# A graph layer on one core: banks of their own for spread scores and turned probabilities, sums one step later, expansion three steps ahead

## What is computed

```python
h = relu(layernorm(x))                     # 6250 nodes, 256 features
q, k, v = h @ wq + bq, h @ wk + bk, h @ wv + bv
scores = sum(q[dst] * k[src], -1) / 16 + (edge_weight * we + be)   # 200000 edges, sorted by dst
attn = softmax of scores over the edges of one dst
out = segment_sum(v[src] * attn, dst)
y = layernorm(h + out + h @ ws + bs)       # with g1, b1
return x + layernorm(y + ffn(y))           # with g2, b2
```

## Time and profile before

| | us |
|---|---|
| median of 3 runs | 2336.25 (2335.91 to 2336.41) |
| span of the profiled execution | 3211.3 |

### The profile page before, as it was taken

One profiled execution on the slowest core, in us unless ns is written; L12 is line 12 of the kernel. 1 busy time (PEld: TensorE's weight loads), 2 busy tenths in 40 slices (PEclk: granted clock), 3 DMA queues, 4 the chain that ended last, 5 costly groups with the idle time before them and its releaser, 6 DMA issues. The chain is left out here.

```text
span 3211.3 us, 68474 instructions
## 1 busy us (share of the span) xinstructions
PE 2427.3 (76%) x14747; PEld 1996.1 (62%) x14748; DVE 1767.6 (55%) x7372; ACT 1193.2 (37%) x2930; POOL 1635.5 (51%) x1828
## 2 busy tenths in 40 slices
PE   7577677777777777777777777777777777778998
PEld 5455556556555556565656566665666666657897
DVE  7454455555555545554555555555555555556787
ACT  6333333333333333333333333333333333334666
POOL 5355565555555545555554555555555445441154
PEclk8898899899899989998998999899988899999999
DMA  7233333333233323333233333332333233222222
GB/s 231 76 103 103 99 105 101 103 98 107 90 100 100 96 86 101 97 98 96 90 102 92 96 90 96 96 98 87 96 96 100 87 92 95 83 93 71 82 74 68
DMA packets 148148, 311.29 MB, mean 97 GB/s; under 512 B 33566, under 2 KB 84625, under 8 KB 148104
## 3 DMA queue, kind: packets, MB, share of 16 engines
q0 software_dynamic: 75264, 205.62, 21.5%
q1 hardware_dynamic: 54718, 90.19, 8.6%
q10 hardware_dynamic: 18122, 14.96, 1.5%
HBM read 290.21 MB, written 20.43 MB: 97 GB/s over the span
## 5 line engine op out<-in xcount | busy, mean ns | idle before, releaser
L488 POOL DMA_INDIRECT work<-h_rows,idx x1536 | 1457.3, 949 | 1339.9 <-SPq L372 956.2
L1079 PE MATMUL bank<-work 128*128 x3520 | 939.0, 412 | 24.5 <-issue 17.7
L1011 PE MATMUL bank<-q,onehot 128*128 x5304 | 804.6, 291 | 1.2 <-DVE work L832 0.7
L1079 PEld LDWEIGHTS bank<-work 128*128 128x128 f32 x3520 | 700.1, 211 | 146.8 <-issue 45.2
L886 DVE CUSTOM_DVE_ANT_0 work<-bank,work 128x512 f32<-128x512 f32 x440 | 330.5, 751 | 778.7 <-remote 476.4
L622 ACT COPY work<-bank 128x256 f32<-128x256 f32 x880 | 295.0, 376 | 1182.6 <-remote 812.8
L832 DVE SCALAR_TENSOR_TENSOR work<-bank,work 128x257 bf16<-128x257 f32 x1764 | 651.6, 425 | 143.5 <-PE bank L1011 44.2
L1017 PE MATMUL bank<-ident,work 128*128 128x128 f32 x1764 | 307.4, 302 | 500.5 <-ACT work L622 313.3
L1011 PEld LDWEIGHTS bank<-q,onehot 128*128 128x128 bf16 x5304 | 549.5, 104 | 85.4 <-issue 1.7
L1017 PEld LDWEIGHTS bank<-ident,work 128*128 128x128 f32 x1764 | 212.8, 148 | 578.0 <-ACT work L622 442.4
L1066 PE MATMUL bank<-ident,work 128*128 128x128 f32 x1760 | 283.6, 285 | 191.8 <-ACT work L619 182.8
(11 more groups left out here) (195 smaller groups left out, 1519.5 us busy)
## 6 DMA issues: line engine op xcount, KB each, us to landing
dst_words<-dst_short SPq DMA_DIRECT2D x99, 512.0 KB
work<-h_rows,idx POOLq DMA_INDIRECT x1568
bias<-h_rows ACTq DMA_DIRECT2D x56, 128.0 KB
r_rows<-bias ACTq DMA_DIRECT2D x55, 128.0 KB
work<-r_rows SPq DMA_DIRECT2D x49, 128.0 KB, 2.3
h_rows<-acc SPq DMA_DIRECT2D x12, 512.0 KB, 6.6
work<-in_x SPq DMA_DIRECT2D x12, 512.0 KB, 3.5
out<-work SPq DMA_DIRECT2D x48, 128.0 KB, 1.7
```

Of the source, the lines that this page charges most:

```text
L488: pool.indirect_dma_start(rows[:, u, j, 0:D], None, h_rows, bass.IndirectOffsetOnAxis(idx[:, half, u * J + j:u * J + j + 1], 0)).then_inc( ...
L1011: last = nc.tensor.matmul(banks[j][:, 0:D1], onehot[:, k, j, :], q3[:, bass.ds(b, 1), c, 0:D1], start=(c == 0), stop=(c == 2))
L1079: last = nc.tensor.matmul(banks[6 + k][:, 0:D1], probs[:, j, :], rows[:, bass.ds(slot, 1), j, :], start=(j == 2), stop=(j == 1))
```

## The change

The edge stage is ordered anew. The lines that matter:

```diff
-        masked = part(C)
+        masked = part(2 * C).rearrange("p (k n) -> p k n", k=2)
         probsT = masked
+        probs_odd = part(C).rearrange("p (j n) -> p j n", j=J)
+        probs = [probs_even, probs_odd]
...
-                        for half in (1, 0):
-                            act.wait_ge(turned, s * 2 + (2 - half))
-                            nc.scalar.copy(probs[:, 2 * half:2 * half + 2, :]..., banks[5 - half][:, 0:2 * P]).then_inc(probs_done, 1)
                         prepare(s + 2, k)
+                        act.wait_ge(turned, s + 1)
+                        nc.scalar.copy(probs[k][:]..., banks[5][:]).then_inc(probs_done, 1)
...
                 dve.wait_ge(lo_done, B)
+                nc.vector.memset(probs[1], 0.0).then_inc(probs_done, 1)
                 edge_scores(ahead[0], 0, 0, 0)
                 dve.wait_ge(outside_done, 1)
                 mark(place_of_mark(ahead[2]), 0)
+                edge_scores(ahead[1], 0, 1, 1)
+                dve.wait_ge(outside_done, 2)
+                mark(place_of_mark(ahead[3]), 1)
...
-                        edge_scores(step_at(regs[u + 1]), r, s + 1, 1 - k, meanwhile)
+                        edge_scores(step_at(regs[u + 2]), r, s + 2, k, meanwhile)
...
+                        if steps == U and u in (2, 3):
+                            dve.wait_ge(hTe_copied, ...)
+                        if steps == U and u in (5, 6):
+                            dve.wait_ge(r_copied, ...)
-                        add_sums(s, 1 - k, held if u == 0 else blocks[u - 1])
+                        add_sums(s, u + 2, held[u] if u < 2 else blocks[u - 2])
...
# PE, one step
-                        pe.wait_ge(exp_done, s + 1)
-                        (turn the probabilities of s, in two halves)
-                        pe.wait_ge(onehot_done, s + (S + 3))
-                        pe.wait_ge(dotted, s * 2 + 3)
-                        expand_q(k, 0, b)
-                        pe.wait_ge(scored, s + 2)
-                        pe.wait_ge(probs_done, s * 2 + 1)
-                        spread_scores(1 - k)
-                        pe.wait_ge(dotted, s * 2 + 4)
-                        expand_q(k, 1, b)
-                        (sums of s; wait for the second copy between the halves)
+                        pe.wait_ge(masked_done, s + 1)
+                        pe.wait_ge(scored, s + 2)
+                        spread_scores(1 - k)
+                        pe.wait_ge(probs_done, s + 1)
+                        sum_rows(1 - k, 1, slot)
+                        pe.wait_ge(exp_done, s + 1)
+                        turn_probs(k)
+                        pe.wait_ge(onehot_done, s + (S + 4))
+                        pe.wait_ge(dotted, s * 2 + 5)
+                        expand_q(1 - k, 0, b)
+                        pe.wait_ge(dotted, s * 2 + 6)
+                        expand_q(1 - k, 1, b)
+                        sum_rows(1 - k, 0, slot)
# PE, behind the loop
+                sum_rows(1, 1, slot)
+                sum_rows(1, 0, slot)
```

More of the change, by code:

```diff
@@ L266, in gnn_layer @@
         used[0] = EDGE_FIRST
[L267 removed]
+        masked = part(2 * C).rearrange("p (k n) -> p k n", k=2)
         probsT = masked
[L269 to L270 removed]
+        probs_even = part(C).rearrange("p (j n) -> p j n", j=J)
+        products = [part((D1 + 1) // 2, BF16)] + [norms[:, k * (D1 + 1) // 2:(k + 1) * (D1 + 1) // 2].bitcast(BF16) for k in range(J - 1)]
         assert used[0] <= PLAN_FIRST
@@ L831, in edge_scores @@
                         for j in (2 * half, 2 * half + 1):
-                            last = nc.vector.scalar_tensor_tensor(out=product[:, j, 0:D1], in0=banks[j][:, 0:D1], scalar=SCALE, in1=rows[:, bass.ds(slot, 1), j, :],
+                            last = nc.vector.scalar_tensor_tensor(out=products[j][:, 0:D1], in0=banks[j][:, 0:D1], scalar=SCALE, in1=rows[:, bass.ds(slot, 1), j, :],
                                                                   op0=ALU.mult, op1=ALU.mult, accum_out=dots[:, k, j:j + 1])
@@ L908, in _ @@
                     trip(0, n, HALF)
-                add_sums(dve.snap(steps_done, min_val=0, max_val=B * TP), 1, dve.snap(held, min_val=0, max_val=B))
+                for u in range(2):
+                    add_sums(dve.snap(steps_done, min_val=0, max_val=B * TP) + u, u + 2, dve.snap(held[u], min_val=0, max_val=B))
             @block.tensor
@@ new lines, in turn_probs, with sum_rows @@
+                def turn_probs(k):
+                    for j in range(J):
+                        last = nc.tensor.transpose(banks[5][:, j * P:(j + 1) * P], probsT[:, k, j * P:(j + 1) * P], ident[:])
+                    last.then_inc(turned, 1)
+                def sum_rows(k, half, slot):
+                    for j in (2 * half, 2 * half + 1):
+                        last = nc.tensor.matmul(banks[6 + k][:, 0:D1], probs[k][:, j, :], rows[:, bass.ds(slot, 1), j, :], start=(j == 2), stop=(j == 1))
+                    if half == 0:
+                        last.then_inc(summed, 1)
@@ L1060, in trip @@
+                    slot = pe.snap(slot_before, min_val=0, max_val=S - 1)
                     for u in range(steps):
                         s, k = first + u, u % 2
-                        b, slot = block_of(pe, step_of[u + 2]), slot_of(pe, step_of[u] >> (BLOCKS.bit_length() - 1))
-                        pe.wait_ge(exp_done, s + 1)
-                        for half in (1, 0):
-                            for j in range(2):
-                                last = nc.tensor.transpose(banks[5 - half][:, j * P:(j + 1) * P], probsT[:, (2 * half + j) * P:(2 * half + j + 1) * P], ident[:])
-                            last.then_inc(turned, 1)
```

201 lines of the change are left out of this document (118 added, 83 removed).

## The result

The changed kernel takes **2626.97 us** (median of 4 runs, 2624.39 to 2628.34) beside 2336.08 for the kernel before: ratio 1.1247, 95% interval 1.1231 to 1.1263. It is 291 us slower where 10 were forecast.

A forecast was written before the change was run, and what follows sets the result against it. The prediction took POOL's gathers to set the pace in the unrecorded run. The median of 2336.25 us plus 5.8 at the start and 4.3 at the end made 2346 us (+ 0.43%), range 2300 to 2356.

The forecast's parts named there:

- the masks on registers: DVE's masks on register values in the loop: 0 to 0.5 us each with the new waits, under 0.9 us slack; taken as 0.
- the four cases: POOL leads (0.60); late hand-overs cost something (0.15); hand-overs set the pace (0.17); new waits weigh more (0.08).
- DVE's new waits for the copies: DVE's four new waits in 8 steps for h block copies: 0 where POOL leads, at most 110 us, taken as 0.
- rival D: New waits in the loop weigh more, two of 8 steps above 5 us: 27 us and more, 2360 or above; chance 0.08.
- POOL leads, 1933 us of gathers: Edge loop: POOL's 1536 gathers at 1.251 us plus 48 index copies take 1933 us and set the unrecorded pace; chance 0.60.
- rival B: POOL leads early, late blocks lose about 20 us to hand-overs; the change gives 2336 to 2342, or 2326; chance 0.15.
- C: The gather's 1.25 us is swollen by recording and hand-overs set the pace; 2267, or 2190 to 2210; chance 0.17.
- C's other half: Loop steps of 4.25 to 4.30 us net of the projection, 0.30 to 0.35 over PE's 3.95, set by hand-overs.
- 2184 to 2206: Whole kernel by PE alone: 2206 us, or 2184 without first-stage holds; something else takes 130 to 152 us.
- Start, + 5.8 us: Before POOL's first loop gather: 3.1 us of DVE work ahead of the loop and 2.7 from maximum to gather, paid in full.
- End, + 4.3 us: After the last chunk lands: 11.1 us of PE work in place of 6.8.
- The 875 us of "recording": Profiled execution spans 3211.3 us, the median run 2336.25; claimed that recording slows PE's hand-overs and hides POOL's lead.

The follow-up runs named there:

- b_masks_4: Kernel before with only the changed kernel's masks on register values, old order, on a chip of the 2336 kind: 2539.73 us, ratio 1.0877.
- b_masks_pad: Kernel before with the masks plus 99 net filler instructions in one piece, on the 3209 kind: ratio 1.0029.
- a_pad_2: Changed kernel plus 68 filler instructions ahead of DVE's loop, on the 2336 kind: 2402.65 us, ratio 1.0279.
- a_pad_early_2: Changed kernel plus 68 filler instructions, with ACT's copies of the h block ahead of its wait for the turning, 2336 kind: 2361.34 us, ratio 1.0103.
- a_free_early_3: Changed kernel with the h block copies ahead of ACT's wait and 67 filler instructions where DVE idles, 2336 kind: 2352.21 us, ratio 1.0073.
- b_g3: Kernel before with masks and 99 net filler instructions, each chunk's fourth gather left out in the loop: 2271.27 us, ratio 0.9715.
- b_masks_3: Repeat on the 3209 kind of the kernel before with only the masks on register values; the two repeats there gave ratios 1.0416 and 1.0404.
- a_pad_part: Changed kernel plus 36 filler instructions ahead of DVE's loop in place of 68, on the 3209 kind: 3308.46 us, ratio 1.0291.
- b_masks: Kernel before with only the changed kernel's masks on register values, old order, first run on the 3209 kind: 3344.4 us, ratio 1.0434.

## Why the prediction was wrong

**The step that failed** is the one that put the masks on registers at nothing. It asked how long DVE takes to issue them and what lies beside that. That part stands to a few us where it was measured: with filler the old order with masks is 1.003 to 1.004 of before (3209 kind; the intervals run from 0.9994 to 1.0073). It did not ask what they do to the length of the code. The body of DVE's loop grew from 321 to 370 recorded instructions, 38 of these 49 by the masks, and moved; behind 54 of its 55 jumps DVE then stands still, 3.13 us in the median. The hold and what follows it are 5.0 us a trip where POOL does not lead. None of the four cases had this, so the range was not merely too narrow: a case was missing. The number to ask about was on the page of before, 24 packets on queue 14 for the whole program: its loop fetches next to nothing (one packet behind its first jump, in the profile of the 3209 kind). That it could be made to fetch at every jump by 38 more instructions the page does not say; the runs show it, with 295 packets in b_masks_4 and 25 in b_masks_pad.

Where the 291 us went, on the 2336 kind:

| from | to | us | shown by |
|---|---|---|---|
| changed, 2627.0 | a_pad_2, 2402.7 | 224 | the hold and what follows it, net of the filler's own cost |
| a_pad_2, 2402.7 | a_pad_early_2, 2361.3 | 41 | `add_sums` behind the copies |
| a_pad_early_2, 2361.3 | a_free_early_3, 2352.2 | 9 | the filler in one piece (7 by the ratios to before; the first gather starts at 136.97 and 129.54) |
| a_free_early_3, 2352.2 | before, 2334.8 to 2336.1 | 16 to 17 | later start and end, the rest open (below) |

**DVE's new waits for the copies** were put at 0, up to 110 us at most, "0 where POOL leads". The mechanism was right and the size was not: the waits are 4.15 us a trip in place of at most 2, since ACT reaches the copies behind its wait for the turning, and they cost 41 us, inside the 110 but not 0. This is the prediction's rival D: without the hold the changed kernel would be at about 2395 (an estimate: 2403 less the filler's 7 to 9), within D's "2360 or above" and above the stated range's 2356. So even without the hold the forecast would have missed. The early copies show that it could have been avoided.

**POOL leads, 1933 us of gathers**: right as a sum, 1931 measured in a_free_early_3, at 1.25 us start to start. Wrong as the state of the changed kernel, in which POOL waits 280 us for slots between 400 and 2200 us. And in a_free_early_3 it holds only up to about 1600 us: the last chunk lies landed for some 16 us (18 less the 2.3 of the landing), about the 20 us that rival B gives to the late blocks. The rival that the spacing is swollen by recording (C) falls: it is 1.25 us in every profile with all gathers, also on the 2336 kind, where the profiled execution is as fast as the others. C's other half, a step of 4.25 to 4.30 us without the projection, is half right: b_g3 steps in 34.3/8 = 4.29 us with the projection (0.15), where 4.1 were taken from the stretch behind the last gather. That is 0.19 too little and not 0.30 to 0.35. Nearly all of it is the last step of a trip, 5.13 us for 3.95, and that stretch lies in the last trip and has no such step. (C's limit of 1.2 us for a gather leaves the projection out as well; with it the step would be 4.40 to 4.45 and the limit 1.24 to 1.25, so that even a true 1.25 was too near to it to speak for POOL against the hand-overs.) So PE without POOL in its way is not at 2184 to 2206 but at 2271, and what POOL adds is 65 us, not 130 to 152.

**Start, + 5.8 us**: the first gather of the loop is at 129.54 in a_free_early_3 and at 123.54 in b_masks_4 (2336 kind), + 6.0. The sum is right, its parts are not quite: from the first maximum (118.12 and 116.19) to the first gather are 11.42 and 7.35, + 4.1 where 2.7 were forecast, and the first maximum comes 1.9 later, not 3.1. **End, + 4.3 us**: from the last maximum to the end of the span are 2351.2 - 2085.5 = 265.7 in the one and 2539.3 - 2278.1 = 261.2 in the other, + 4.5. Counted as the prediction does, from the last chunk's dot products, they are 271.0 and 263.6, + 7.4 (+ 5.1 beside the 265.9 of the profile of before). So the two terms behind the forecast's 10 us have the right size, in part by luck. a_free_early_3 is 17.4 above its before, so 4 to 7 are left over. They may be the masks (0.3% of 2336 is 7), the loop's first trips or the late ones, in which POOL does not lead; there is no profile of before on the 2336 kind, and no run tells which.

**The 875 us of "recording"** were another kind of chip: that recording slows this kernel, as the section on the time before has it, does not hold. What the prediction read as an effect of recording is real there: hand-overs from PE to ACT are held among gathers. The same program on both kinds, ACT's waits from 400 to 2200 us, b_masks_4 (2336 kind) first, then b_masks_3 (3209 kind):

```profile
ACT work L623 <- DVE work L891: 628.5, 366, 7.6
ACT work L627 <- PE bank L1071: 369.9, 359, 2.3
...
ACT work L623 <- DVE work L891: 483.8, 237, 8.1
ACT work L627 <- remote: 449.2, 128, 9.2
ACT work L627 <- PE bank L1071: 200.4, 158, 3.5
```

On the 3209 kind ACT's copy waits 449 us, up to 9.2 us at a time, for something that the profile only calls remote, and 200 us for PE. The stretch holds 266 steps there and 366 on the 2336 kind; per step the copy waits 2.5 us and 1.0 (with its "issue" rows of 26.0 and 8.3 us), which is most of the 1.8 us by which the step is longer. The conclusion drawn from the difference (take the rates from a free stretch, judge the whole by POOL's spacing) happened to give the right bound all the same.

## What to carry to other kernels

Before costing an edit inside a loop, count the instructions of each engine between two jumps, and compare the page's instruction packets before and after: here five a trip came with a hold at every jump, 224 us of 2627. Instructions of no effect ahead of the loop are a cheap test, and here a cure. When an engine leads, as POOL with its gathers up to about 1600 us, more slack elsewhere buys nothing there, but what a change adds at the start is paid in full; and that an engine never waits does not show that it leads, so look also at who waits for its results. And where a profile's span and the median disagree by a third, ask first whether they are from the same chip.

## What the runs showed of the hardware

- The packets on queue 14 hold 8.2 KB (2.41 MB in 294), and in the changed kernel's loop one comes every 117 to 137 recorded instructions of DVE along the straight code, where no hold is seen; with 36 instructions of filler (a_pad_part) they come 33 to 40 instructions earlier in the body. Behind the jump DVE's next instruction comes after 3.1 us (median; 3.2 and up to 5.3 in b_masks_4), and after 0.28 us where the loop brings no packets.
- One and the same loop body of DVE, of 370 recorded instructions, takes five packets a trip (53 of 54 trips in the changed kernel) or none (53 of 54 in a_pad_2), by where it begins: 0 or 36 instructions of filler ahead of it gave 294 packets, 68 gave 25. With a body of 359 it was 295 without filler (b_masks_4) and 25 with it (b_masks_pad).
- PE's body has about 610 recorded instructions, more than DVE's, and nothing is fetched for it in the loop: with filler in DVE's code alone neither queue brings a packet in the later trips, and behind PE's jumps in the changed kernel the next instruction comes after 0.05 us.
- In a hold of 4 us in which PE was busy 0.45 us the granted clock fell to 0.50 and stayed there for 6.8 us, likewise behind 54 jumps of the changed kernel. In b_masks_4 it was 6.8 us in 31 trips and 3.4 in 23; in a_pad_2, without the hold, the whole loop has four such stretches of 3.4 us. Hold and low clock together cost 5.0 us a trip (40.9 in the changed kernel, 35.9 in a_pad_2).
- Chips differ: the same program (the old order with masks) takes 2539.7 us on one kind (b_masks_4) and 3342 to 3355 on the other (b_masks and its repeats). The difference lies in the edge stage: from the last maximum to the end are 261.2 us in b_masks_4 and 261.3 in b_masks_3.
